# A four-layer graph network on one core: in layer 1 the negated pieces move from ScalarE to VectorE, the first score row comes in quarters, and the neighbour count compares 1024 columns at a time

## The reference

```python
x = _layernorm(x + _L0_gnn_ref(x, L0_gnn_x2, L0_gnn_v, adj))   # 8-head attention masked by adj
x = _layernorm(x + _L1_gnn_ref(x, adj, W, a, gamma, beta))     # graph attention + batch norm
x = _layernorm(x + _L2_gnn_ref(x, adj, W_nb, b_nb, W_line, b_line, 64))  # mean of the first 64 neighbours
x = _layernorm(x + _L3_gnn_ref(x, adj, ...))                   # mean of all neighbours
```

```python
e = leaky_relu(s_dst[:, None, :] + s_src[None, :, :], 0.2)
attn = softmax(where(adj > 0, e, -9e15), axis=1)
h_prime = einsum('ijh,jhd->ihd', attn, Wh)
h_prime = relu(gamma * (h_prime - mean) * rsqrt(var + eps) + beta)    # over the nodes
```

## Time and profile before

| | |
|---|---|
| median of 3 runs | 873.53 us (872.39 to 874.77) |
| profiled execution | 873.28 us, span 871.6 us |
| PE busy | 814.6 us, 93% |
| DVE busy | 688.7 us, 79% |
| ACT busy | 581.2 us, 67% |
| loop over the heads of layer 1 | from 448.6 to 637.9 us |
| comparisons on ACT, line 1262 | 87, mean 1988 ns |
| masks on DVE, line 1166 | 65, mean 1203 ns |

### The profile page before, as it was taken

One profiled execution on the slowest core, in us unless ns is written; L12 is line 12 of the kernel. 1 busy time (PEld: TensorE's weight loads), 2 busy tenths in 40 slices (PEclk: granted clock), 3 DMA queues, 4 the chain that ended last, 5 costly groups with the idle time before them and its releaser, 6 DMA issues. The chain is left out here.

```text
span 871.6 us, 18880 instructions
## 1 busy us (share of the span) xinstructions
PE 814.6 (93%) x7820; PEld 510.7 (59%) x7820; DVE 688.7 (79%) x1045; ACT 581.2 (67%) x608; POOL 149.4 (17%) x287
## 2 busy tenths in 40 slices
PE   3999999999999999995869999999988999999997
PEld 1344444344444444442559999999944557777786
DVE  7587979898998989896889999999853595555454
ACT  6798989896777767671479999999959731111000
POOL 3501012653110100000520000000001352111122
PEclk9999999999999999997979999999998999999999
DMA  8965354393211010002121110011000000000011
GB/s 292 263 196 165 110 149 131 109 242 88 84 25 49 13 49 1 13 1 66 42 100 52 52 40 30 34 51 52 3 1 1 1 1 1 1 1 1 2 49 49
DMA packets 28183, 56.85 MB, mean 65 GB/s; under 512 B 5760, under 2 KB 9984, under 8 KB 26560
## 3 DMA queue, kind: packets, MB, share of 16 engines
q1 hardware_dynamic: 23968, 46.19, 17.2%
q0 software_dynamic: 4128, 9.44, 4.1%
HBM read 38.70 MB, written 2.23 MB: 47 GB/s over the span
## 5 line engine op out<-in xcount | busy, mean ns | idle before, releaser
L484 ACT ACTIVATE ex<-scores_ps,shift 128x1024 f32<-128x1024 f32 x256 | 262.5, 1130 | 77.3 <-PE scores_ps L344 69.4
L555 DVE TENSOR_TENSOR esum<-esum,ex 128x1024 f32<-128x1024 f32 x192 | 223.0, 1212 | 6.1 <-ACT ex L484 6.1
L340 PE MATMUL scores_ps<-qst,kst 128*128 128x512 f32 x512 | 201.6, 475 | 2.5 <-ACT ex L484 1.8
L994 PE MATMUL banks<-fx,pos 128*128 128x132 f16 x2048 | 161.7, 223 | 9.4 <-DVE fx L1097 5.4
L1262 ACT ACTIVATE steps<-a_all,big_b_head 128x2048 fp8e5<-128x2048 f32 x87 | 166.2, 1988 | 0.0
L344 PE MATMUL scores_ps<-edge,negI 128*128 128x512 fp8e5 x512 | 155.3, 385 | 0.0
L340 PEld LDWEIGHTS scores_ps<-qst,kst 128*128 128x128 f32 x512 | 90.2, 189 | 69.6 <-ACT ex L484 18.2
L994 PEld LDWEIGHTS banks<-fx,pos 128*128 128x128 fp8e5 x2048 | 122.2, 98 | 11.5 <-issue 8.4
L1001 PE MATMUL banks<-fm,edge 128*128 128x66 f16 x2048 | 104.8, 194 | 0.0
L1001 PEld LDWEIGHTS banks<-fm,edge 128*128 128x128 fp8e5 x2048 | 87.3, 98 | 0.0
L1166 DVE TENSOR_TENSOR pos<-steps,edge 128x1024 int32<-128x1024 int32 (+1 forms) x65 | 76.9, 1203 | 11.1 <-PE banks L994 5.5
(11 more groups left out here) (209 smaller groups left out, 933.4 us busy)
## 6 DMA issues: line engine op xcount, KB each, us to landing
adj_raw<-in_adjT_dram SPq DMA_DIRECT2D x32, 512.0 KB, 5.2
a_all<-score_rows_dram SPq DMA_DIRECT2D x8, 1024.0 KB, 4.6
kst<-high_low SPq DMA_DIRECT2D x56, 64.0 KB, 4.5
kst<-high_low POOLq DMA_DIRECT2D x56, 64.0 KB, 4.9
qst<-high_low POOLq DMA_DIRECT2D x56, 64.0 KB, 2.2
qst<-high_low SPq DMA_DIRECT2D x56, 64.0 KB, 3.6
ex<-in_x2T_dram SPq DMA_DIRECT2D x2, 1024.0 KB, 6.8
ex<-in_xT_dram SPq DMA_DIRECT2D x2, 1024.0 KB, 8.8
```

The costliest lines, as they stand in the source:

```text
L340: nc.tensor.matmul(to, kst[:, h, jt * P:(jt + 1) * P], qst[:, it % 2, h, :], start=True, stop=False)
L484: nc.scalar.activation(ex[:, s % ER, h, :], scores_ps[:, u % SR, :], ACT.Exp, bias=shift[:, it // NC * HG + h:it // NC * HG + h + 1], scal ...
L555: nc.vector.tensor_tensor(esum[:, h, :], other, ex[:, s % ER, h, :], ALU.add).then_inc(summed, 1)
L994: done = nc.tensor.matmul(place(half, i), pos[:, group_of(h, k, half) % GR, jt % GU, i * P:(i + 1) * P], fx[:, e, jt].rearrange("p k r c - ...
```

## The change

`OWN` gives VectorE one more comparison in the last head. The first score row is broadcast in four quarters, each as soon as it is written. The scalars for head 0 (`bigh`) are made ahead. Before the first unit VectorE makes the low pieces of the first 8 tiles ahead of its comparisons, and those of the other 8 after the first mask. The negation of heads 1 to 7 leaves ScalarE's `cut_part` and becomes a VectorE instruction between the two masks of k = 3 (`leave(..., 2)`). `scale_weights` goes to the end of ScalarE's loop. `AHEAD` is 2, not 3, and a comparison of the count spans two banks.

```diff
-    OWN = [(2, 2, 1, 1)] + [(1, 2, 1, 1)] * (H - 2) + [(1, 1, 1, 0)]
+    OWN = [(2, 2, 1, 1)] + [(1, 2, 1, 1)] * (H - 2) + [(1, 1, 1, 1)]
...
+        def loads_to(h):
+            return 16 * (h // 2 + (GS if h % 2 == 0 else 1))
...
                     sp.dma_start(score_rows[:, at], arow[:, at]).then_inc(written, 16)
-                sp.wait_ge(written, 16 * GS)
-                sp.dma_start(aall[:, 0, :], score_rows[H:H + 1, :].broadcast_to([P, N])).then_inc(a_landed[0], 16)
+                    sp.wait_ge(written, 16 * (g + 1))
+                    sp.dma_start(aall[:, 0, at], score_rows[H:H + 1, at].broadcast_to([P, CW])).then_inc(a_landed[0], 16)
...
                     if h:
-                        pe.wait_ge(cut, h * CS + 1)
+                        pe.wait_ge(negated, h + 2)
...
                 step(nc.vector.tensor_scalar(bigb[:], b, BIG, None, ALU.mult))
+                nc.vector.tensor_scalar(bigh[:, 0, :], bigb[:, :, 0], 1.0, None, ALU.mult).then_inc(bigh_ready, 1)
...
                 def leave(h, e, r):
                     if r == 0:
-                        dve.wait_ge(cut, h * CS - 1)
+                        dve.wait_ge(cut, h)
+                        dve.wait_ge(negated, h + 1)
...
+                    else:
+                        dve.wait_ge(rest_step, h * RS + 3)
+                        nc.vector.tensor_scalar(fx[:, e, :, 1], fm[:, e], -1.0, None, ALU.mult).then_inc(negated, 1)
...
-                for r in range(2):
-                    for ab in range(2):
-                        leave_first(r, ab)
-                    if r == 0:
-                        big_head(0, 0)
-                        own_steps(0, 0)
-                        mask(0, 0, 0, 0, OWN[0][0])
+                leave_first(0, 0)
+                leave_first(0, 1)
+                leave_first(1, 0)
+                own_steps(0, 0)
+                mask(0, 0, 0, 0, OWN[0][0])
+                leave_first(1, 1)
...
+                        if k == 3 and not last:
+                            leave(h + 1, 1 - e, 2)
...
-                        if k == 2 and h == 2:
-                            pair.scale_weights(act)
-                        if k >= 2 and not last:
-                            cut_part(h + 1, 1 - e, k - 2)
+                        if k == 2 and not last:
+                            cut_high(h + 1, 1 - e)
+                    if last:
+                        pair.scale_weights(act)
...
-    AHEAD = 3
+    AHEAD = 2
...
-        for c in range(NC):
-            act.wait_ge(self.cum, t * NC + c + 1)
-            self.nc.scalar.activation(self.kept(t)[:, c * NC:(c + 1) * NC, :],
-                                      ps[:, c, :].rearrange("p (i n) -> p i n", n=P), ACT.Sigmoid,
+        for c in range(0, NC, 2):
+            act.wait_ge(self.cum, t * NC + c + 2)
+            self.nc.scalar.activation(self.kept(t)[:, c * NC:(c + 2) * NC, :],
+                                      ps[:, c:c + 2, :].rearrange("p c (i n) -> p (c i) n", n=P), ACT.Sigmoid,
                                       bias=self.limit[:], scale=-2.0 * self.SHARP, saturate=False
-                                      ).then_inc(self.kept_ready, 1)
+                                      ).then_inc(self.kept_ready, 2)
```

More of the change, by code:

```diff
@@ L871, in layer1 @@
         own_ready = S.sem("own_ready")
-        RS, CS = 2, 2
+        RS = 2
         DONE0, HALF0, EV0, POS0 = GR * GU, 3, 2, T
@@ L1104, in leave @@
                                                 ).then_inc(rest_step, 1)
[L1105 to L1109, removed]
+                    elif r == 1:
+                        dve.wait_ge(cut, h + 1)
+                        for k in range(2):
+                            ins = low_piece(e, slice(0, T), k)
+                        ins.then_inc(rest_step, 1)
+                    else:
+                        dve.wait_ge(rest_step, h * RS + 3)
+                        nc.vector.tensor_scalar(fx[:, e, :, 1], fm[:, e], -1.0, None, ALU.mult).then_inc(negated, 1)
                 def join_pieces(h, half):
@@ L1152, in own_steps @@
                     if k == 0:
-                        dve.wait_ge(a_landed[h % 2], (h // 2 + 1) * 16)
+                        dve.wait_ge(a_landed[h % 2], loads_to(h))
                     dve.wait_ge(pos_ready, (pair_of(h, k) - SLOTS + 1) * 2 * GU + POS0)
@@ L1244, in _, with cut_high @@
                 nc.scalar.activation(efac[:], efac[:], ACT.Exp)
[L1246 to L1254, removed]
+                def cut_high(h, e):
+                    act.wait_ge(half_done, h * 2 + (-2 + HALF0))
+                    act.wait_ge(rest_step, h * RS + 2)
+                    nc.scalar.copy(fm[:, e, :, 0, :], rest[:, 1])
+                    nc.scalar.copy(fx[:, e, :, 0, 0, :], rest[:, 0]).then_inc(cut, 1)
                 def compare(h, e, k):
                     if k == 0:
-                        act.wait_ge(a_landed[e], (h // 2 + 1) * 16)
+                        act.wait_ge(a_landed[e], loads_to(h))
                         act.wait_ge(bigh_ready, h + 1)
@@ L1265, in compare_first @@
                 def compare_first(half):
-                    act.wait_ge(a_landed[0], 16)
+                    act.wait_ge(a_landed[0], loads_to(0))
                     act.wait_ge(bigh_ready, 1)
```

## The result

The changed kernel took 869.56 us (median of 19 runs), the kernel before 874.14 in as many beside it: ratio 0.9942, 95% interval 0.9932 to 0.9952, which is 5.1 us less (the two medians alone differ by 4.6). One of the 19 runs took 1666.19 us; it is not in the ratio. The profiled execution took 870.34 us, span 868.6. It is one of the slower ones: the last scores of layer 1 were kept 1.8 us later than in the profile before. 1.1 us of that is there when layer 1 begins, the other 0.7 comes with the first three tiles of its preparation, which both kernels compute alike.

The account below looks back on a forecast made before the run. ScalarE was taken to pace the heads at 23.11 us, with TensorE next at 22.4. Loop -5.9 and tail +0.5 give -5.4 us: 867.9 profiled, 868.1 against the median; range 866.3 to 869.8, upper end pulled to 871.5.

Parts of the forecast that it names:

- The pace of the heads: Loop over heads: ScalarE's 23.11 us a head gives way to TensorE's 22.4, with VectorE at 22.4 to 22.6.
- the late masks of head 2: Loop, head 2: VectorE's one-off powers of the weights don't fit, so its masks come late, 0.3 us.
- The 7% and the upper end of 871.5: Loop: 7% chance of a rival in which the negation costs VectorE more; rivals pull the range's top to 871.5 us.
- The loop's end: End of the loop over heads: at 632.0 in place of 637.88, 5.9 us earlier, with 0.4 us of waits.
- The start: Before the loop: TensorE's first unit 1.4 us earlier, 1.02 from reordered low pieces and negation, 0.38 from the earlier row.
- nothing else waits behind them: Start, SP's queue: four writes and four reads in turn delay nothing else, so the row lands at 442.8, not 444.1.
- rival 3: Start: the row isn't earlier and the second mask waits; start wins 0.5 us at most, 868.8 to 869.5 us; 5%.
- the clock that it assumed: Loop's start: TensorE's drop to 1.2 GHz stays where it was, ending at 456.3; without it 1.8 us more are won.
- The count: Count and tail after the loop: a loss of 0.5 us in all, between -0.9 and +1.5.
- The chain of a pair: Count: successive comparisons of a bank pair wait for each other, 2.25 to 2.3 us a tile, nearly cancelling the instruction gain.
- a tile earlier: 2.3 us: Count: with AHEAD 2 layer 1's block ends 2.3 us earlier, offset by 2.3 us later between the batch norm's applications.
- rival 4: Tail: TensorE stays at 1.2 GHz through the ScalarE-paced tiles, 1.1 us a tile more, 878 us with nine; 4%.

Follow-up runs that it names:

- experiment 1: The kernel before with only the negation of heads 1 to 7 moved from ScalarE to VectorE; 868.69 us, ratio 0.9944.
- experiment 2: The changed kernel with the negation of heads 1 to 7 back on ScalarE; 873.47 us, ratio 0.9993.
- experiment 8: The changed kernel with two more negations of like size a head on VectorE; 871.46 us, ratio 0.9974.
- Experiment 3: The changed kernel with its first score row read back in one transfer after all four writes; 868.37 us, ratio 0.9931.
- experiment 4: The changed kernel with the first score row's last half read in one transfer after the last write; 868.60 us, ratio 0.9939.
- experiment 5: The changed kernel with a one-column Sigmoid on ScalarE after the scaling of the weights, loading the function table early; 868.05 us, ratio 0.9934.
- experiment 6: The changed kernel with the count as before, AHEAD 3 and single banks of 512 columns; 866.66 us, ratio 0.9922.
- experiment 7: The changed kernel with single banks of 512 columns and still two tiles ahead; 867.51 us, ratio 0.9937.

## Why the prediction was right

**The pace of the heads.** Right, and shown from both sides by experiments 1 and 2: ScalarE's 23.11, then TensorE's 22.44 (forecast 22.4), with VectorE just under it (22.27 by experiment 8; forecast 22.4 to 22.6). The negation adds 0.34 us on VectorE (0.36 forecast), and the late masks of head 2 cost 0.28 us (22.72; 0.3 forecast). So VectorE did not become the pace. The 7% and the upper end of 871.5 had left room for a negation that costs VectorE much more; no run shows such a cost. By the Trainium skill (VectorE: DVE Perf Modes, "What auto-detection actually checks") the engine takes its 4x mode for a single source and a destination that are both 16-bit with a step of one, lie in SBUF, and have outermost dimensions that are even or equal. The trace agrees: 528 elements more took 0.428 - 0.297 = 0.131 us more, 4.0 elements a nanosecond.

**The loop's end.** Forecast 5.9 us earlier, measured 6.0; so close a match is luck, as two errors cancel. The start won 0.9 us and not 1.4: the step that failed is "nothing else waits behind them" about SP's queue. I let the last write take what it took before and only shortened its read; in the changed kernel the write came behind a read. Experiment 3 shows that the quarters gave nothing, experiment 4 that without the read in between 0.35 to 0.8 us are there. This was the first half of rival 3, the row that isn't earlier; its second half did not come: the unit that waits for the second mask starts 0.9 us nearer to "kept" (453.50 - 439.8 against 452.53 - 437.9 in the earlier trace rows).

On the other side TensorE's clock at the start was 1.2 GHz for 3.4 us and not 10.2 as I had left it. The row of that stretch in the profile after, as the earlier trace rows:

```profile
449.30:452.70 3.40, 2.80 (x32) 2.67 (x32) 3.37 (x6) 3.40 (x3) 1.07 (x1) 0.51 0.08 31
```

In experiments 1, 3, 4 and 5 this drop lasted 10.2, 10.2, 6.8 and 10.2 us, and their loops took 184.1, 184.6, 183.9 and 184.9: it differs from run to run. In the four traces with the new start and a drop of 10.2 us (experiments 3, 5, 6 and 7) the loop ends 5.2 to 5.9 us nearer to "kept" than before. So the forecast of 5.9 is at the upper end of what the change gives with the clock that it assumed.

**The count.** The chain of a pair was forecast at 2.25 to 2.3 us a tile; 654.15 to 656.45 is 2.30, so the saved instruction brings nothing. But from the loop's end on 1.2 us were lost where 0.5 was forecast. The step that failed is that the block of layer 1 would end "a tile earlier: 2.3 us": with a tile less, its first transpose of the tail came 0.9 us later after the loop's end (10.9 for 10.0). What was missed is the table load, which the forecast has nowhere: 1.28 us of it went onto the path, and 0.28 more is the wait for two banks in place of one (first comparison at 0.69 in experiment 5, at 0.41 with single banks). Even where the clock held, in experiment 3, the tail starts only 0.6 us earlier (9.4). The rest is a drop of TensorE's clock during the count:

```profile
637.00:640.40 3.40, 3.40 (x9) 1.16 (x8) 0.93 (x3) 1.89 (x3) 0.00 (x0) 0.50 0.00 0
```

TensorE had idled 2.1 us while ScalarE loaded the table and compared. The drop lasted 3.4 us and cost about 1.4 us up to the tail's start (10.9 against 9.4 in experiment 3, the same code there without a drop). It looks like the beginning of rival 4, but it isn't shown that the idle time called it: the same 2.1 us stand in experiments 2, 3 and 8, with no drop in the count. Not all of load and drop stays in the end: the tail before had two drops of 3.4 us, this one has none after the count.

**The sum.** -5.4 forecast, -5.1 measured by the ratio; 868.1 against a median of 869.56, with a kernel before that itself ran at 874.14 and not 873.53 in the longer series. The main term, the negation, was right in mechanism and size. That the sum came out so near is in part luck: the start won 0.5 too little, the count lost more than forecast, and the clock, which differs from run to run, gave some back in the profiled one.

## What to carry to other kernels

Where three engines are within 5% of each other, find the one whose work has next to no gap from one round to the next (here ScalarE, 0.11 us a head, where VectorE waited 1.1). Take a microsecond from that one, and the gain is at most the distance to the next engine, 0.67 us a head here. Work taken off elsewhere is worth little until then: the other edits of this change came to 0.6 us together. Before a phase that starts with another function on ScalarE, look where the table load lands.

## What the runs showed of the hardware that was not expected

*A table load can wait.* With a bank at a time the comparison carries its wait itself, and the load stands free ahead of it (experiments 6 and 7, and the kernel before). With pairs, which count their semaphore up by two, the wait is an instruction of its own ahead of the load: the trace after has 32 EVENT_SEMAPHORE instructions of ScalarE at that wait's line, the trace before has none. That the count by two is what parts them wasn't tried by itself. The Trainium skill (ScalarE: Activation LUTs, "What ACT_TABLE_LOAD costs") gives 1283 ns for the load, as here, and about 1380 ns more for a drain. The traces show no such drain, and here the measurement decides: the comparison starts 1.29 us after the start of the load, and in experiment 5, where the load stands straight behind the scaling of the weights, the whole step is no longer either (625.38 to 626.67).

*A small write behind a large read.* The last quarter's write (32 KB) was issued 0.4 us after a read of 256 KB on the same queue and took 3.1 us from its issue to that of the read that depends on it; the writes without a read just ahead took 1.6. In the six traces with quarters it landed after 2.8 to 3.1 us.
